# Plain mamba units: the output row scale moves from VectorE to ScalarE, and the residual becomes one VectorE addition

## The reference

```python
h = x
for i in range(N_LAYERS):                      # 2
    res = h
    h = _layernorm(h, ln_w[i], ln_b[i])
    h = _mamba2(h, in_proj_w[i], ...)          # 256 -> 512 channels, 8 heads of 64, state 64
    h = h + res
x = _layernorm(x + h)
x = _layernorm(x + _L0_ffn_ref(x, ...))        # 8 experts, 2 for each token
```

```python
y = y * jax.nn.silu(z)
y = y * jax.lax.rsqrt(jnp.mean(y * y, -1, keepdims=True) + EPS) * rms_w
return y @ out_w.T
```

## Time and profile before

| | |
|---|---|
| median of 3 runs | 1420.89 us (1419.91 to 1421.42) |
| span of the profiled execution, first to last instruction | 1418.7 us |
| time of the profiled execution itself | not given apart from the three runs |
| median less span | 2.2 us |
| a plain unit, start of one `end_b` to the next | 40 to 41 us |
| plain units (u = 1 to 8) | about 98 to 424 us of the span |
| TensorE's granted clock, mean | 0.965 |

### The profile page before, as it was taken

How to read it: one execution, slowest core, us unless ns; L and a number is a source line. 1 busy time by engine, 2 the same in 40 slices (tenths; PEclk the granted TensorE clock), 3 DMA queues, 4 the chain that set the end, 5 groups by cost and what they waited for, 6 DMA issues and landing times.

```text
span 1418.7 us, 40444 instructions
## 1 busy us (share of the span) xinstructions
PE 1272.5 (90%) x13336; PEld 1050.7 (74%) x13337; DVE 1090.1 (77%) x2560; ACT 804.2 (57%) x1861; POOL 791.7 (56%) x751
## 2 busy tenths in 40 slices
PE   4889999999999999999888799999999999999970
PEld 2456666666667666666678799999999999999960
DVE  4889999999999999899967877565566656565536
ACT  4667666666666776667545344444454544444436
POOL 3467666767675877788774615234072406152772
PEclk9899999999999999999968999999999999999996
DMA  6213432333443233322235231303012312202594
GB/s 211 81 31 120 135 109 93 96 119 119 135 135 120 84 113 117 123 88 81 87 146 189 72 121 34 121 27 122 30 54 94 105 51 76 72 30 63 134 210 162
DMA packets 90547, 145.73 MB, mean 103 GB/s; under 512 B 9376, under 2 KB 73376, under 8 KB 90336
## 3 DMA queue, kind: packets, MB, share of 16 engines
q1 hardware_dynamic: 75104, 97.03, 21.4%
q0 software_dynamic: 15072, 46.51, 11.2%
q10 hardware_dynamic: 288, 1.19, 0.2%
HBM read 103.03 MB, written 41.67 MB: 102 GB/s over the span
## 4 chain that ended last, share of the span: by engine, by line
PE 48%; DVE 25%; issue 12%; POOL 6%; ACT 5%; DMA 1%; DVEq 1%; SPq 0%; ACTq 0%; POOLq 0%
PE pe L1101 12%; PE pa L1101 12%; PE py L1126 11%; DVE arena L1691 5%; DVE arena L1730 4%; POOL arena L2631 3%; PE pa L676 2%; DVE arena L1738 2%; PE pm L853 2%; PE py L815 2%; DVE arena L1757 2%; DVE arena L1744 1%; PE pt L835 1%; DVE arena L1664 1%; DVE arena L1645 1%
## 5 line engine op out<-in xcount | busy, mean ns | idle before, releaser
L1101 PE MATMUL pe<-arena 128*128 128x128 f16 x3408 | 219.4, 220 | 26.0 <-issue 26.0
L1101 PEld LDWEIGHTS pe<-arena 128*128 128x128 f16 x3408 | 203.4, 98 | 31.3 <-issue 30.6
L1101 PE MATMUL pa<-arena 128*128 128x128 f16 x3408 | 218.8, 220 | 0.0
L1553 ACT ACTIVATE arena<-pe,arena 128x128 f32<-128x128 f32 x568 | 162.0, 371 | 79.8 <-PE pe L1101 78.9
L1101 PEld LDWEIGHTS pa<-arena 128*128 128x128 f16 x3408 | 201.5, 98 | 0.0
L1126 PE MATMUL py<-arena 128*128 (+1 forms) x1704 | 197.7, 273 | 1.3 <-DVE arena L2337 0.9
L1691 DVE SCALAR_TENSOR_TENSOR arena<-pa,arena 128x511 f32<-128x511 f32 (+2 forms) x240 | 178.9, 746 | 11.6 <-ACT arena L1199 5.5
L1126 PEld LDWEIGHTS py<-arena 128*128 128x128 f16 x1704 | 163.4, 98 | 19.6 <-issue 1.8
L2300 DVE SCALAR_TENSOR_TENSOR pm<-pa,arena 128x128 f32<-128x128 f32 x284 | 80.5, 352 | 98.7 <-ACT arena L1553 88.0
L1730 DVE TENSOR_TENSOR_SCAN arena<-arena,pe 128x512 f32<-128x512 f32 x128 | 148.8, 1204 | 3.2 <-issue 1.8
L2531 POOL TENSOR_SCALAR arena<-arena 128x1536 f16<-128x1536 f32 (+2 forms) x35 | 42.6, 1218 | 189.3 <-DVE arena L2337 184.1
(11 more groups left out here) (309 smaller groups left out, 2539.5 us busy)
## 6 DMA issues: line engine op xcount, KB each, us to landing
arena<-step_rows SPq DMA_DIRECT2D x64, 512.0 KB, 6.3
arena<-in_w_exp POOLq DMA_DIRECT2D x32, 768.0 KB, 4.8
arena<-queue SPq DMA_DIRECT2D x74, 129.5 KB, 2.1
answer<-arena SPq DMA_DIRECT2D x71, 128.0 KB, 1.7
arena<-in_x SPq DMA_DIRECT2D x16, 512.0 KB, 6.2
answer<-zeros SPq DMA_DIRECT2D x10, 512.0 KB, 4.8
arena<-h SPq DMA_DIRECT2D x9, 512.0 KB, 5.5
h<-arena SPq DMA_DIRECT2D x8, 512.0 KB, 3.0
```

The lines of the kernel that those rows point to most:

```text
L1101: ins = pe.matmul(bank[:, f * P:(f + 1) * P], w_split[:, p, hl, d * 2 * FF + col:d * 2 * FF + col + P], x[:, r, d, :], start=(n == 0), sto ...
L1553: ins = e.activation(sg[:, half, f, :], GATE[half][:, f * P:(f + 1) * P], ACT.Silu, bias=b1a[:, bass.ds(ex_, 1), ff], scale=1.0 / S1)
```

## The change

```diff
 # ScalarE, plain(st)
                 conv_first(st, "c4")
                 conv_first(st, "c0")
                 first_state(c[0])
+                end_scale(st)
                 chunk_c(c[0])
                 steps(st)
                 conv_silu(st, "c4")
 # VectorE
-            def end_b(st):
-                wq = 1 - st.q
-                dve.wait_ge(srs_ready, st.u)
-                dve.wait_ge(out_free, NK * st.u)
-                dve.wait_ge(hres_in[wq], 16 * ((st.h + 1) if wq == 0 else st.h))
-                for k in range(NK):
-                    ins = dve.scalar_tensor_tensor(ob[:, wq, k, :], ob[:, wq, k, :], srs[:, k:k + 1],
-                                                   hres[:, wq, k, :], ALU.mult, ALU.add)
-                ins.then_inc(h_ready, 1)
             def end_add(st):
                 wq = 1 - st.q
-                dve.wait_ge(h_scaled, st.u - NB)
+                dve.wait_ge(h_scaled, st.u)
                 dve.wait_ge(hres_in[wq], 16 * ((st.h + 1) if wq == 0 else st.h))
                 dve.tensor_tensor(ob[:, wq], ob[:, wq], hres[:, wq], ALU.add).then_inc(h_ready, 1)
 # VectorE, plain(st)
                 weigh(st)
-                end_b(st)
+                end_add(st)
                 g_low(c[0])
```

## The result

| | before | after |
|---|---|---|
| median of 8 runs each, us | 1419.88 (1417.44 to 1422.71) | 1426.99 (1423.17 to 1436.92) |
| profiled execution: span, us | 1418.7 | 1424.2 |
| start of the last `weigh` (unit 14), us | 669.36 | 674.49 |

The ratio of after to before is 1.0049, 95% interval 1.0031 to 1.0067: the kernel is 7 us slower. 1418.1 was predicted, with a range up to 1421.3, and slower had a chance of 0.10. The profiled execution's own time is 1426.02, 1.8 us above its span. The granted clock is the same within 0.001 (0.966 after, 0.965 before).

A forecast was written before the change was run, and what follows sets the result against it. In plain units DVE was taken to lead, with ACT's `conv_first` next to bind; 8 x 0.35 = 2.8 us off 1420.9 gave 1418.1 us (span 1415.9). Range 1415.0 to 1421.3.

The forecast's parts named there:

- What bounds the plain unit: Second half of a plain unit: DVE leads, and what delays or advances it there moves the other engines equally.
- `end_scale` hidden: ACT's four added scalings, 2.07 us at most, fit its idle wait for PE, ending some 1.6 us early; cost nothing.
- 1.46 us out of DVE: Plain unit's end: one addition holding DVE 1.14 us replaces `end_b`'s 2.60, so DVE's work shrinks by 1.46 us.
- `add_xd` at 2.2: POOL's `add_xd` of chunk 1, meeting the longer addition at the port, takes about 2.2 us.
- the taps bound by `acc_init`: `taps` of c1 wait for ACT's `acc_init`, ending at 195.00, so start about 195.03 instead of 195.38.
- 0.35 us through: Per plain unit, 0.35 of DVE's 1.46 us come through; about 0.5 us become a new wait for ACT.
- the 2.8 of the sum: Total gain over the eight plain units: 8 x 0.35 = 2.8 us.
- The table: Rival, ACT: scaling forces extra table loads, 0.93 us a unit, 7.4 us slower, 1428.3 us; chance 0.09 with other ACT stalls.
- Everything after unit 8 starts 2.8 us sooner and is otherwise unchanged.: Everything behind the plain units: the 2.8 us gain is carried to the end of the kernel with nothing else changing.
- The rival of the meeting at the port: Plain units' `dt_last` against `x_w`: four collisions vanish, 1415.1 us (chance 0.08), or four appear, 1421.1 (within a shared 0.18).
- 0.05 us was little: Unit 3: `dt_last` starts 0.05 us before `x_w`; that distance was expected to stay, though called little.
- Its sign of being wrong: Whole kernel: among the signs that the forecast is wrong, the number of long L1682 (`dt_last`) changes.

The follow-up runs named there:

- e6: e2's kernel, with the plain units' residual addition on VectorE replaced by a one-column memset: 1413.02 us, ratio to before 0.9950.
- e2: Changed kernel, with GpSimd's `x_w` of chunk 1 waiting for VectorE's `dt_last` in units 0 to 14: 1416.04 us, ratio to before 0.9966.
- e3: Kernel before the change, with GpSimd's `x_w` of chunk 1 waiting for VectorE's `dt_last`: 1417.58 us, ratio to before 0.9972.
- e1: Changed kernel plus three one-column VectorE memsets ahead of `end_add` in every plain unit: 1419.71 us, ratio to before 0.9989.
- e5: Changed kernel plus twelve one-column VectorE memsets in unit 8 alone: 1418.86 us against 1419.61, ratio to before 0.9993.
- e4: Kernel before the change plus three one-column VectorE memsets behind `end_b` in every plain unit: 1420.19 us, ratio to before 0.9991.

## Why the prediction was wrong, step by step

- *What bounds the plain unit, and `end_scale` hidden.* Right. Its margin was 1.6 us by the forecast and is 1.89.
- *1.46 us out of DVE, `add_xd` at 2.2, the taps bound by `acc_init`, 0.35 us through.* Right: `end_add` holds DVE 1.14, `add_xd` takes 2.23, the taps wait 0.38 for ACT (about 0.5 was forecast), and the units but for the seventh are 0.33 to 0.35 shorter. Together they give 1.93 us instead of the 2.8 of the sum, since the seventh loses 0.45. The forecast end of `add_xd`, 193.60, is 2.35 us after `end_b`'s start; measured 192.16 - 189.82 = 2.34. e6 shows that ACT binds.
- *The table.* Did not come: ACT has 35 table loads up to 760 us in both kernels.
- *"Everything after unit 8 starts 2.8 us sooner and is otherwise unchanged."* This step failed. At unit 10 `weigh` was 3.0 us sooner; at unit 14 it was 5.1 us later. The sentence gives no row of the routed units' queues on DVE and POOL. They are sensitive in just the way that the rival on the port describes, and had the rows been read there, they would have shown `dt_last` 70 ns behind a scatter with two TENSOR_TENSOR of POOL right behind it.
- *The rival of the meeting at the port.* Right in its mechanism and in 0.75 us for a plain unit (e2, e3); 0.05 us was little indeed: in unit 7 `dt_last` went from 0.14 us ahead of `x_w` to 0.10 behind it and took 0.99 instead of 0.19, 0.45 us net. But it was placed in plain units alone and priced by the meetings behind the start of `x_w`. In units 11 and 13 `dt_last` starts ahead of `x_w`'s row, beside the scatter, and is held until `x_dt` too is done: 2.5 us on DVE, then PE waits 2.6 us behind `gated`, and the interval grows by 2.95. Two of them and what comes behind make 8.2 us; the rival's price for the worst case was 3.0. Its sign of being wrong did show: the long `dt_last` went from six (units 2, 4, 6, 8, 9, 12) to nine (7, 11 and 13 besides).
- *The cause of the lateness.* The prediction treats a step that gets shorter as a gain or nothing. That an edit of the stream moves the stalls behind it was not considered. e1 and e5 show that the number of instructions ahead decides whether the 0.41 us are there; e4 that this can't be foretold from the number alone.

Open: what DVE waits for in such a stall; why `dt_last` moved in unit 7 alone of the plain ones; why the intervals behind a collision lose a further 1.37 and 0.89 us, which no run took apart; and part of the size: the last `weigh` is 5.1 us later than before (5.9, counted from the `weigh` of unit 1), the span 5.5 longer, the medians 7.1 apart. From the last `weigh` to the end it is 746.2 (e5) to 753.1 us (e6) for the same instructions, so that single spans tell less than the intervals do.

## What to carry to other kernels

Where a small VectorE instruction with two SBUF inputs runs within some tenths of a microsecond of GpSimd's work, look at its durations row by row (a median of 194 ns hid those of 940 to 990), and price a meeting by what GpSimd has queued, not only by one instruction. A semaphore that orders the two can be worth more than the change under study: by the medians one wait gave 11 us in the changed kernel and 3.3 in the one before. When an edit changes an engine's instruction count, compare the stages that it does not touch as well, and fill the stream with empty instructions before blaming the edit itself.

## What the runs showed of the hardware

Whether `dt_last` is free goes by how long after the third scatter's start it begins. With `x_w` queued behind the scatter it was free (0.19 us) at 61, 70, 92, 101, 293 and 294 ns, and held for 2.63 to 2.68 us at 413, 417, 445 and 458. With `x_w` waiting for it, it was free at 410, 413, 458 and 461 ns. `x_w`'s row begins only 0.98 us after the scatter's start. So here a GpSimd TENSOR_TENSOR that is next in its queue held VectorE from more than half a microsecond before its row begins, and until the one behind it was done. The rows of POOL are rough in this profile, so that the true start of `x_w` may lie ahead of its row.

Two in a row do not always do that. In units 9 and 12 `x_dt` follows `x_w` at once as well, but `dt_last` starts 0.05 to 0.11 us behind `x_w`'s row, and it ends 0.05 us after `x_w`, in 0.98 to 1.03 us. Unit 12, after:

```profile
563.80 1.03 POOL L2593 TENSOR_TENSOR arena<-arena 128x512 f32<-128x512 f32 x1 [0.59 <-ACT arena L1242]
564.80 1.03 POOL L2585 TENSOR_TENSOR arena<-arena 128x512 f32<-128x512 f32 x1
...
563.86 1.03 DVE L1683 TENSOR_TENSOR arena<-arena 128x32 f32<-128x32 f32 x1
```

Nor is it enough that VectorE comes first: in unit 3 `dt_last` starts 0.05 us ahead of `x_w`'s row, with GpSimd idle until then, and is free. The expensive meeting needs the scatter running, `x_w` queued behind it, and `dt_last` late beside it. Why VectorE then gets no turn between `x_w` and `x_dt` stays open.

The Trainium skill, "SBUF — State Buffer", section SBUF: two separate sides, says that when a VectorE instruction with two SBUF inputs and a GpSimd one that reads SBUF meet, whichever starts first has the shared pair for its whole instruction, and the other blocks fully. Units 9 and 12 agree: the hold ends with `x_w`. In units 11 and 13 the rule, by the start times of the rows, would have let `dt_last` through at 413 ns, 0.58 us ahead of `x_w`, and a hold would have ended with `x_w`; the measurement differs in both and decides.

DVE stalls for 0.41 us on straight code with nothing shown as the cause, at places that move when instructions far ahead are added or removed (0.41 at 505.26 after; none there in e1 and e5, but 0.38 at 540.30 in e5). The cost of the stall itself is small, 0.35 us in an interval of e2; with the collision that it set off the interval grew by 2.95.
